# Row maxima of the attention scores from 64-row matmuls in pairs, and the low parts of the probabilities on one engine

## What is computed

```
xn = rms_norm(x, gamma)
q, k, v = split(xn @ w_qkv)            # 16 heads, 64 wide
q = q * 64 ** -0.5
sim = einsum('bhid,bhjd->bhij', q, k)  # 2048 x 2048 per head
attn = softmax(sim, axis=-1)
out = einsum('bhij,bhjd->bhid', attn, v)
x = x + out_all_heads @ w_out
```

## Time and profile before

| what | value |
|---|---|
| median of three runs | 2309.75 us (2306.97 to 2312.76) |
| profiled execution: its span, the only time the page gives of it | 2302.3 us |
| PE busy, modelled ends | 2142.9 us, 93% |
| DVE busy | 1805.1 us, 78% |
| ACT busy | 1587.2 us, 69% |
| POOL busy | 1004.2 us, 44% |
| mean granted TensorE clock | 0.955 of full speed |

### The profile page before, as it was taken

The page is one execution under the profiler, slowest core; times in us unless marked ns, Lnnn a source line. Parts: engine busy times, 40 slices in busy tenths (PEclk is TensorE's granted clock), DMA queues, the critical chain, the costliest instruction groups (busy, mean ns, idle before and its releaser), DMA issues.

```text
span 2302.3 us, 32776 instructions
## 1 busy us (share of the span) xinstructions
PE 2142.9 (93%) x9032; PEld 1504.7 (65%) x9032; DVE 1805.1 (78%) x2535; ACT 1587.2 (69%) x1898; POOL 1004.2 (44%) x636
## 2 busy tenths in 40 slices
PE   6999459998779999999999999999999999999997
PEld 4777237776647666666766666666666667666654
DVE  5888867886588888887888788788888878888555
ACT  4666426664427877777787777777777787777873
POOL 1000100003025566565565656556565655656672
PEclk7999769998679999999999999999999999999998
DMA  3210003110000000000000000000000000000000
GB/s 115 63 49 19 0 0 75 43 30 15 1 3 1 12 1 14 3 10 10 7 12 4 12 3 10 15 1 12 5 11 3 10 15 1 12 2 10 11 1 19
DMA packets 25125, 36.59 MB, mean 16 GB/s; under 512 B 11807, under 2 KB 14239, under 8 KB 23711
## 3 DMA queue, kind: packets, MB, share of 16 engines
q1 hardware_dynamic: 24958, 34.56, 5.8%
HBM read 32.99 MB, written 1.43 MB: 15 GB/s over the span
## 4 chain that ended last, share of the span: by engine, by line
PE 73%; DVE 13%; issue 7%; ACT 4%; POOL 2%; DVEq 0%; DMA 0%; ACTq 0%; POOLq 0%
PE ps L478 14%; PE ps L480 13%; PE ps L479 13%; PE ps L586 8%; PE ps L608 8%; PE ps L609 8%; DVE m_part L1219 2%; PE ps L460 2%; DVE p_l L1249 2%; POOL p_l L380 1%; ACT p_raw L926 1%; DVE m_part L1331 1%; DVE kb L1207 1%; PE ps L613 1%; PE ps L453 1%
## 5 line engine op out<-in xcount | busy, mean ns | idle before, releaser
L380 POOL TENSOR_TENSOR p_l<-p_raw,p_h 128x512 fp32r<-128x512 f32 (+1 forms) x512 | 836.9, 1635 | 651.3 <-ACT p_h L930 645.4
L1219 DVE TENSOR_REDUCE m_part<-ps 128x1 f32<-128x512 f32 x960 | 643.3, 685 | 191.0 <-PE ps L586 186.1
L926 ACT ACTIVATE p_raw<-ps 128x1024 f32<-128x1024 f32 x512 | 524.9, 1025 | 308.6 <-PE ps L609 283.6
L930 ACT ACTIVATE p_h<-p_raw 128x1024 fp32r<-128x1024 f32 x512 | 543.0, 1061 | 27.5
L1249 DVE TENSOR_TENSOR p_l<-p_raw,p_h 128x512 fp32r<-128x512 f32 x384 | 431.0, 1123 | 63.9 <-ACT p_h L930 49.8
L608 PE MATMUL ps<-qa,ka 128*128 128x512 f32 x1024 | 418.3, 408 | 7.4 <-DMA qb<-m_t 7.4
L478 PE MATMUL ps<-p_h,v_l 128*65 128x512 f32 x1024 | 404.4, 395 | 7.2 <-DVE p_l L1249 6.1
L609 PE MATMUL ps<-qb,kb 65*128 65x512 f32 x1024 | 407.5, 398 | 0.0
L479 PE MATMUL ps<-p_h,v_h 128*65 128x512 f32 x1024 | 402.6, 393 | 0.0
L480 PE MATMUL ps<-p_l,v_h 128*65 128x512 f32 x1024 | 402.4, 393 | 0.0
L586 PE MATMUL ps<-ka,qa 128*128 128x512 f32 x960 | 381.9, 405 | 8.0 <-DVE m_part L1219 5.6
(11 more groups left out here) (177 smaller groups left out, 2730.8 us busy)
## 6 DMA issues: line engine op xcount, KB each, us to landing
big<-g_scratch SPq DMA_DIRECT2D x64, 256.0 KB, 3.2
xnp<-r_scratch SPq DMA_DIRECT2D x15, 512.0 KB, 4.8
big<-in_w1T SPq DMA_DIRECT2D x1, 2048.0 KB, 9.0
big<-in_w2T SPq DMA_DIRECT2D x1, 2048.0 KB, 13.5
x<-in_xT SPq DMA_DIRECT2D x4, 256.0 KB, 3.6
qk_raw<-in_w_qkv SPq DMA_DIRECT2D x32, 32.0 KB, 1.9
out_xT<-x SPq DMA_DIRECT2D x4, 256.0 KB, 2.0
wv_raw<-in_w_qkv SPq DMA_DIRECT2D x8, 64.0 KB, 1.9
```

What stands on the lines that cost most here:

```text
L380: nc.gpsimd.tensor_tensor(p_l[:, g % 4, tiles, :], p_raw[:, g % 4, tiles, :], p_h[:, g % 4, tiles, :].bitcast(fp32), ALU.subtract).then_in ...
L926: af(p_raw[:, g % 4, :, :], ps[:, 2 * (g % 2):2 * (g % 2) + 2, :], ACT.Exp).then_inc(exp_done, 1)
L930: af(p_h[:, g % 4, :, :], p_raw[:, g % 4, :, :], ACT.Copy).then_inc(ph_done, 1)
L1219: nc.vector.tensor_reduce(m_part[:, ds(c, 1), it:it + 1].rearrange("p a t -> p (a t)"), ps[:, 4 + it % 2, :], AX.X, ALU.max).then_inc(s_ma ...
```

## The change

Three edits, with the semaphores that follow from them.

1. A pair of tiles takes the place of two tiles. `score_pair` multiplies the high part of q with the high part of k alone, 64 rows deep: the even tile from partitions 0 to 63 (`qa`, `kb`) into bank 4, the odd tile from partitions 64 to 127 (`qa`, `ka`) into bank 5. The maximum is used as a shift only, and the same shift stands in numerator and denominator. `MAXIMA_PAIRS` sets how many pairs fall in a group: mostly one, behind `scores_t`. A pair waits until the maximum of the pair before it is done.
2. DVE's `maximum` reads both banks in one instruction, 128x1024 to 128x2.
3. DVE makes the whole low part of each group, 128x1024; POOL makes none. POOL keeps `low_v` and `scale`.

```diff
-POOL_GROUPS = (2, 4)
-MAXIMA_TILES = ((0, 2, 2, 3, 2, 2, 3, 2), (2,) * 8, (2,) * 8, (3, 3, 3, 2, 2, 2, 1, 0))
+MAXIMA_PAIRS = ((0, 1, 1, 2, 1, 1, 1, 1), (1,) * 8, (1,) * 8, (2, 1, 1, 1, 1, 1, 1, 0))
...
-            def score_tile(head, par, c, it):
-
-                if it < 2:
-                    pe.wait_ge(s_max, PRIME + NC * NT * head + NT * c)
-                else:
-                    pe.wait_ge(s_max, PRIME + NC * NT * head + NT * c + it - 1)
-                mm(ps[:, 4 + it % 2, :], qa[par][:, it * 128:it * 128 + 128], ka[par][:, ds(c * CH, CH)],
-                   start=True, stop=True).then_inc(s_ps, 1)
+            def score_pair(head, par, c, ip):
+
+                pe.wait_ge(s_max, PRIME + NC * NT * head + NT * c + 2 * ip)
+                even, odd = 2 * ip * 128, 2 * ip * 128 + 128
+                mm(ps[:, 4, :], qa[par][0:DH, even:even + 128], kb[par][0:DH, ds(c * CH, CH)],
+                   start=True, stop=True)
+                mm(ps[:, 5, :], qa[par][DH:128, odd:odd + 128], ka[par][DH:128, ds(c * CH, CH)],
+                   start=True, stop=True).then_inc(s_ps, 2)
...
-            def maximum(head, c, it):
-                dve.wait_ge(s_ps, NC * NT * head + NT * c + it + 1)
-                nc.vector.tensor_reduce(m_part[:, ds(c, 1), it:it + 1].rearrange("p a t -> p (a t)"),
-                                        ps[:, 4 + it % 2, :], AX.X, ALU.max).then_inc(s_max, 1)
+            def maximum(head, c, ip):
+                dve.wait_ge(s_ps, NC * NT * head + NT * c + 2 * ip + 2)
+                nc.vector.tensor_reduce(m_part[:, ds(c, 1), 2 * ip:2 * ip + 2].rearrange("p a t -> p (a t)"),
+                                        ps[:, 4:6, :], AX.X, ALU.max).then_inc(s_max, 2)
...
-                if g not in POOL_GROUPS:
-                    n = GROUPS * (NC * head + c) + g
-                    dve.wait_ge(ph_done, n + 1)
-                    if not start or g >= 4:
-                        dve.wait_ge(pv_done, n - 3)
-                    tt(p_l[:, g % 4, 0, :], p_raw[:, g % 4, 0, :], p_h[:, g % 4, 0, :].bitcast(fp32),
-                       ALU.subtract).then_inc(pl_even, 1)
+                n = GROUPS * (NC * head + c) + g
+                dve.wait_ge(ph_done, n + 1)
+                if not start or g >= 4:
+                    dve.wait_ge(pv_done, n - 3)
+                tt(p_l[:, g % 4, :, :], p_raw[:, g % 4, :, :], p_h[:, g % 4, :, :].bitcast(fp32),
+                   ALU.subtract).then_inc(pl_done, 1)
```

More of the change, by code:

```diff
@@ L41 @@
 TURN_BANK, END_BANK = 4, 5
-POOL_GROUPS = (2, 4)
-SCALE_GROUP = 3
 V_STEPS = NT // 2
@@ L190, in macaron_kernel @@
         m_ready, mt_ps, mt_done, m_loaded = sem("m_ready"), sem("mt_ps"), sem("mt_done"), sem("m_loaded")
-        st_ps, exp_done, ph_done, pl_even, pl_odd, pv_done = (
-            sem("st_ps"), sem("exp_done"), sem("ph_done"), sem("pl_even"), sem("pl_odd"), sem("pv_done"))
+        st_ps, exp_done, ph_done, pl_done, pv_done = (
+            sem("st_ps"), sem("exp_done"), sem("ph_done"), sem("pl_done"), sem("pv_done"))
         s_ps, s_max = sem("s_ps"), sem("s_max")
@@ L221, in low_parts_done @@
                 c, g = c - 1, g + GROUPS
-            own = GROUPS - len(POOL_GROUPS)
-            eng.wait_ge(pl_even, own * (NC * head + c) + sum(i not in POOL_GROUPS for i in range(g + 1)))
-            eng.wait_ge(pl_odd, GROUPS * (NC * head + c) + g + 1)
+            eng.wait_ge(pl_done, GROUPS * (NC * head + c) + g + 1)
         def wait_x(eng, k, c):
@@ L371, in quant_ffn, with low_v, scale @@
                                                 ALU.subtract).then_inc(f_lo, 1)
-            def low_part(head, c, g, start):
-                n = GROUPS * (NC * head + c) + g
-                pool.wait_ge(ph_done, n + 1)
-                if not start or g >= 4:
[L378 to L383, removed]
+            def low_v(head, par):
                 pool.wait_ge(v_hi, head + 1)
-                pool.wait_ge(pl_odd, low_parts)
                 nc.gpsimd.tensor_tensor(v_l[:, par, :, 0:DH], v_raw[:, :, par * DH:par * DH + DH],
                                         v_h[:, par, :, 0:DH].bitcast(fp32), ALU.subtract).then_inc(v_lo, 1)
-            def scale(head, par, piece, low_parts, wait_out=None):
+                pool.wait_ge(v_lo, head + 1)
+            def scale(head, par, piece, wait_out=None):
                 rows = slice(par * DH, par * DH + DH)
@@ L404, in window @@
                 head = 2 * pair + par
[L405 to L408, removed]
                 later = not (isinstance(pair, int) and pair == 0)
[L412 to L423, removed]
+                if par == 0:
+                    low_v(head + 1, 1)
+                for q in range(NC):
+                    if q == 1 and par == 1 and project:
+                        low_v(head + 1, 0)
+                    if scale_before:
+                        scale(head - 1, 1 - par, q, NC * (pair - 1) + q + 1 if par == 1 and later else None)
             def attention():
@@ L637, in spare_free, with next_score_pair @@
                     read(c, g)
[L639 to L646, removed]
+                pairs = iter(range(NT // 2))
+                def next_score_pair():
+                    ip = next(pairs)
+                    if first and ip == 0:
                         pe.wait_ge(hi_done, 12 * (head + 2))
                         pe.wait_ge(lo_done, 8 * (head + 2))
-                    score_tile(head + 1, 1 - par, c, it)
+                        pe.wait_ge(kb_done, NC * (head + 2))
+                    score_pair(head + 1, 1 - par, c, ip)
                 for g in range(GROUPS):
@@ L658, in main_chunk @@
                     scores_t(par, c, g)
[L659 to L665, removed]
+                    if with_next and MAXIMA_PAIRS[c][g] > 0:
+                        next_score_pair()
                     if g < PV_LAG and not first:
@@ L682, in main_chunk @@
                         values(head, par, c, g - PV_LAG)
-                    if with_next:
-                        for _ in range(MAXIMA_TILES[c][g] - before):
-                            next_score_tile()
+                    if with_next and MAXIMA_PAIRS[c][g] > 1:
+                        next_score_pair()
                     n = PROJECTED.get((c, g)) if project else None
@@ L1270, in main_chunk @@
                 start = first_of_all(pair, par, c)
-                tiles = iter(range(NT))
+                pairs = iter(range(NT // 2))
                 for g in range(GROUPS):
@@ L1280, in main_chunk @@
                     if with_next:
-                        for _ in range(MAXIMA_TILES[c][g]):
-                            maximum(head + 1, c, next(tiles))
+                        for _ in range(MAXIMA_PAIRS[c][g]):
+                            maximum(head + 1, c, next(pairs))
                         if (c, g) == (NC - 1, GROUPS - 2):
```

3 lines of the change are left out of this document (removed).

## The result

The changed kernel takes 2382.2 us (median, 2380.1 to 2386.7) against 2311.1 beside it: 1.0312 of before, 95% interval 1.0296 to 1.0329. It is slower, as forecast; the forecast of 2420 us is 38 us too high, and the measured time is nearest to rival 1 (2373). The profiled execution has a span of 2379.4 us, 77.1 more than that of before; the medians are 71.1 apart, since the profiled execution of before was a quick one.

A forecast was written before the change was run, and what follows sets the result against it. PE was taken as the bound, needing about 96 of a head's 99.8 us. Span 2302.3 + 106 for pairs + 5 for waits = 2413 us; with the median 7.5 above the span, forecast 2420 us, range 2350 to 2500.

The forecast's parts named there:

- rival 1: The pair's two halves load and run together on PE: 0.585 us a pair, +58 us, 2373 us in all; 17%.
- The drains: PE empties its array around each pair: entering costs 0.19 us, leaving 0.16 us before values.
- rival 3: No emptying around 64-row matmuls on PE, a pair at one matmul's price, kernel faster at 2242 us; 13%.
- The second load, which I take to follow the first by 0.10: Staggered weight loads within each pair on PE, making a pair 0.685 us, +106 us over 480 pairs.
- That all of it lies on the path: PE being the bound, each pair's extra 0.221 us was added to the span in full, +106 us.
- 0.9 to spare, if DVE is ready: At the pair's single buffer, the maximum is done 0.9 us before PE's next pair is due.
- +5 us for waits: Time in the last chunk above what was counted for PE: 0.3 us a head over 15 heads.
- they lie in the last chunk: PE's waits before the change, about 3 to 4 us a head, placed where low_qk and the maxima meet.
- DVE's prices: A 1024-column maximum takes 1.218 us, a low part 1.22; DVE rises 6.1 us a head to 90.4.
- it doesn't become the bound of a whole head: DVE stays below PE over a head: 88% busy, 90.4 us against PE's need of 103.
- The last chunk: DVE's 28.1 us of work plus 3.3 idle gives 31.4 us; PE's own increase gives 30.5; 28.3 before.
- the sign named for rival 1: In the timeline, the pair's two matmuls, L557 and L559, start less than 0.05 us apart.

The follow-up runs named there:

- single_tiles64: The kernel before with each single tile of the maxima 64 rows deep and standing by itself: 2611.6 us, 1.1306 of before.
- same_rows: The changed kernel with both matmuls of a pair in partitions 0 to 63: 2474.1 us, 1.0718 of before.
- full_pairs_pool: The kernel before with pairs of full 128-row matmuls and one maximum over two banks, low parts still shared by POOL and DVE: 2333.3 us, 1.0102 of before.
- pairs_pool: The kernel before with 64-row pairs and one maximum over two banks, low parts still shared by POOL and DVE: 2350.5 us, 1.0187 of before.
- full_rows: The changed kernel with both matmuls of a pair 128 rows deep again: 2362.3 us, 1.0226 of before.
- early_pairs: The changed kernel with one pair of the last chunk moved ahead of low_qk, from group 6 to group 1: 2383.2 us, 1.0315 of before.
- joint_aligned: The kernel before with both tiles behind the scores, even tile counts, one wait for both banks and two 512-column maxima: 2312.6 us, 1.0013 of before.

## Why the prediction was right, and where it was not

**The drains: mechanism right.** The prediction put entering at 0.19 us and leaving at 0.16 behind a pair followed by values. Measured, the load of L557 comes 0.10 us later than the 0.232 at which it would have streamed, and with 0.10 for loading that is 0.20; from there to the load of L451 are 0.43, that is 0.10 of loading, 0.23 of streaming and 0.10 of emptying, and 0.06 for the next load. A 64-row tile behaves like the 32-row one of the earlier trace rows. This is what kept rival 3 (no emptying, faster) out, and single_tiles64 shows the same cost twice as often.

**"The second load, which I take to follow the first by 0.10": wrong.** Both loads start together, and the pair takes 0.586 us, not 0.685. The term of the sum was +106 us and measured +59: rival 1's figure (0.585 a pair, +58). Its rule from the Trainium skill ("TensorE: Matmul & The Clock Gate", Part 3), loads of different row groups overlap, is what the trace shows: both at 1415.26. I had weighed it down with loads in one and the same row group, which says nothing on two. same_rows bears out the other side: in one row group the second matmul comes 0.34 us behind the first and the pair costs 0.22 more.

**That all of it lies on the path: wrong.** I added the drains to the span in full, since PE was the bound. Taken out, they give back 17 us (full_pairs_pool to pairs_pool) and 20 us (full_rows to the changed kernel) of 59, nearly all of it in the second and third chunks. That the forecast came so near is luck in part: the drains count for somewhat over a quarter of the 71 us, and what I took for small counts for the rest, so one mistake covered another.

**"0.9 to spare, if DVE is ready": the step that failed.** I reckoned the single buffer in the steady state and found room, and booked +5 us for waits. In the steady state the reckoning holds: in the third chunks PE doesn't wait for a maximum at all. But DVE isn't ready in the first chunk either, where the prediction saw no waits, neither before ("they lie in the last chunk") nor after. It and the wide maximum cost 0.8% and 0.9%, about 39 us against two free-running banks, and some 23 against the kernel before, whose tiles stood less well. Two banks let DVE start on the first while PE writes the second and let PE refill the first while DVE reads the second; one instruction over both takes away the first, one wait for both takes away the second. That the wide instruction costs its 0.9% is shown by one pair of kernels that differ in nothing else; the 0.8% is that of the wait together with the even counts. That it works in this way, and which of DVE's neighbours makes a given maximum late, is only argued. PE also waits longer at the start of a head for the row of maxima itself (L581 for `qb<-m_t`, 14.6 us where L608 waited 7.4), which wasn't followed up.

**DVE's prices: right, and edit 3 mis-sized.** 1.220 us for the maximum and 1.225 in the median for the low part, 1.279 in the mean (forecast 1.218 and 1.22), 90.75 us busy a head (forecast 90.4). But "it doesn't become the bound of a whole head" was read as "costs nothing outside the last chunk", and edit 3 costs 25 to 32 us in four comparisons (28 on the kernel before, 25 on tiles_adjacent, 29 from full_pairs_pool to full_rows, 32 from pairs_pool to the changed kernel; 27 to 29 by the ratios), none of it in the third chunks and most in the first and the last. A fuller DVE answers later, though its sum over a head stays below PE's need. That POOL's disturbance would go was right: a low part took 1.215 us for half the columns.

**The last chunk.** Forecast 30.5 to 31.4 us, measured 30.0, with DVE busy for 25.6 of the 28.1 forecast. A head took 104.0 us where 106 to 108 were forecast, and the sign named for rival 1, starts of L557 and L559 closer than 0.05 us, is the one that came. early_pairs moved a pair out of its worst spot and gained nothing.

**The sum.** 2413 us of span forecast, 2379.4 measured: the drains 47 us too high, the rest 13 too low by the span (77.1 - 59 = 18 against 5). By the experiments the shares are different again (about 20 for the drains, 23 for the pairing, 29 for edit 3), because each of them hides a part of the others. Range and sign held.

**A version that beats both.** tiles_adjacent, one number changed from the kernel before, 2295.1 us, 0.9931 (0.9912 to 0.9950): full rows, two banks, two maxima, both tiles behind the scores, low parts shared.

## What to carry to other kernels

Matmuls of few rows that share the array pay for the stay, not for the matmul: some 0.35 us to enter and leave here, whether one or two run inside, so they don't pay when every pair stands between full ones. By these numbers a stay would break even between one pair and two (0.35 us against 0.464 - 0.235 = 0.23 saved by each pair), an estimate that no run here tests. Two buffers that are written, read and freed one by one were worth more than one instruction over both (0.9931 against 1.0102), and the wide instruction saved its engine less than its mean duration promised: compare busy times, not means times counts. Where stages of a loop have different limits, reckon stage by stage: over a whole head DVE had room for its new load here (88% busy by the forecast), and the time was lost in its first and last chunk. And an addition to the engine that bounds isn't an addition to the time when it already waits for another: reckon what it costs beside the waits that it covers, and test it by taking it out of both kernels.

## What was not expected of the hardware

- Loads into different halves of the rows start in the same moment (both 1415.26), and the second 64-row matmul costs 0.01 us (0.586 against 0.576 for one alone). Within one half (same_rows) the second matmul is recorded 0.34 us behind the first.
- A change in PE's order alone (tiles_adjacent) changed how POOL and DVE disturb each other: a mean of 940 ns against 1123 for the same 384 subtractions on DVE, 1732 against 1635 for POOL's 512.
- Two reductions of 512 columns that follow each other on DVE are recorded as overlapping: 616.2 us busy for 960 of 683 ns (joint_aligned).
